# An adaLN and LoRA mixture feed-forward block: full-width warm-up matmuls, one engine for the lower rows' weights, and a last product that is stored bank by bank

## What is computed

```python
# layer 0
y = einsum('bct,bcd->bdt', x, cond_w[itok])          # mixes the 64 rows of each sequence
h = silu(y @ w1.T + b1) * (y @ w2.T + b2)            # up0, up1 (gate and up, 1024 each)
x = x + h @ w3.T + b3                                # down
# layer 1
z = x @ W + (x @ A[itok]) @ B[itok]                  # lin, with rank-16 LoRA
c = softmax((mean_s(z) @ Wq.T) @ keys.T / sqrt(128)) # 8 experts
x = x + z @ W_org.T + sum_e c[e] * (z @ down[e]) @ up[e]   # exp, expup
```

## Time and profile before

| | |
|---|---|
| median of 3 runs | 1001.23 us (1001.08 to 1001.4) |
| the profiled execution | 999.71 us |
| its span in the trace | 998.0 us |
| TensorE matmul busy | 989.2 us, 99% |
| VectorE busy | 743.1 us, 74% |
| ScalarE busy | 391.3 us, 39% |
| GpSimd busy | 39.1 us, 4% |
| granted TensorE clock, mean | 0.999 |

### The profile page before, as it was taken

One profiled execution on the slowest core, in us unless ns is written; L12 is line 12 of the kernel. 1 busy time (PEld: TensorE's weight loads), 2 busy tenths in 40 slices (PEclk: granted clock), 3 DMA queues, 4 the chain that ended last, 5 costly groups with the idle time before them and its releaser, 6 DMA issues.

```text
span 998.0 us, 12355 instructions
## 1 busy us (share of the span) xinstructions
PE 989.2 (99%) x4768; PEld 815.9 (82%) x4768; DVE 743.1 (74%) x578; ACT 391.3 (39%) x349; POOL 39.1 (4%) x65
## 2 busy tenths in 40 slices
PE   8999999999999999999999999999999999999997
PEld 7888888888887888888898888888888878888886
DVE  2977977998866889674436888789885859878641
ACT  7553653543344333331055544543433532424110
POOL 2600000000000000000100000000000000000011
PEclk9999999999999999999999999999999999999999
DMA  9022044034014001425211211521330230031012
GB/s 356 3 91 100 1 166 171 22 108 167 1 43 155 14 1 64 164 90 180 115 43 43 84 43 46 208 85 33 119 145 2 84 127 0 1 106 43 1 64 106
DMA packets 22986, 84.68 MB, mean 85 GB/s; under 512 B 2691, under 2 KB 6803, under 8 KB 17043
## 3 DMA queue, kind: packets, MB, share of 16 engines
q1 hardware_dynamic: 20450, 75.24, 20.8%
q0 software_dynamic: 2400, 8.41, 2.2%
q10 hardware_dynamic: 80, 0.26, 0.1%
HBM read 75.51 MB, written 8.39 MB: 84 GB/s over the span
## 4 chain that ended last, share of the span: by engine, by line
PE 98%; issue 1%; DMA 0%; POOLq 0%; DVE 0%; POOL 0%; SPq 0%
PE banks L653 31%; PE banks L654 31%; PE banks L655 31%; PE banks L749 3%; PE banks L714 2%; PE banks L732 1%; DMA cond_sb<-cond_t_in 0%; DVE r L1017 0%; PE banks L762 0%; POOLq L1166 0%; POOL out_t L631 0%; PE banks L778 0%; POOL mix L464 0%; PE banks L772 0%; SPq L469 0%
## 5 line engine op out<-in xcount | busy, mean ns | idle before, releaser
L653 PE MATMUL banks<-s_hi,t_hi 128*128 128x512 f32 x1360 | 531.7, 391 | 0.0
L654 PE MATMUL banks<-s_lo,t_hi 128*128 128x512 f32 x1360 | 529.5, 389 | 0.0
L655 PE MATMUL banks<-s_hi,t_lo 128*128 128x512 f32 x1360 | 529.2, 389 | 0.0
L653 PEld LDWEIGHTS banks<-s_hi,t_hi 128*128 128x128 f32 x1360 | 255.3, 188 | 56.6 <-issue 3.8
L655 PEld LDWEIGHTS banks<-s_hi,t_lo 128*128 128x128 f32 x1360 | 255.3, 188 | 53.2
L654 PEld LDWEIGHTS banks<-s_lo,t_hi 128*128 128x128 f32 x1360 | 255.3, 188 | 52.5
L1017 DVE TENSOR_TENSOR r<-banks,r 128x1024 f32<-128x1024 f32 x92 | 111.4, 1219 | 97.7 <-PE banks L655 93.1
L919 DVE TENSOR_TENSOR t_lo<-w,t_hi 128x1024 fp32r<-128x1024 f32 x132 | 156.5, 1218 | 5.1 <-ACT t_hi L849 5.1
L830 ACT CAST s_hi<-st 128x2048 fp32r<-128x2048 f32 x40 | 76.5, 1913 | 198.0 <-PE banks L655 145.7
L849 ACT CAST t_hi<-w 128x1024 fp32r<-128x1024 f32 x132 | 133.3, 1048 | 49.0 <-PE banks L655 48.9
L830 ACT CAST s_hi<-r 128x2048 fp32r<-128x2048 f32 x34 | 65.0, 1913 | 203.3 <-PE banks L655 178.2
(11 more groups left out here) (70 smaller groups left out, 356.4 us busy)
## 6 DMA issues: line engine op xcount, KB each, us to landing
w<-w_up_in SPq DMA_DIRECT2D x16, 1024.0 KB, 4.8
w<-w_base_in SPq DMA_DIRECT2D x10, 1024.0 KB, 4.7
w<-w_down_in SPq DMA_DIRECT2D x8, 1024.0 KB, 5.4
r<-x_t_in SPq DMA_DIRECT2D x8, 1024.0 KB, 6.2
w<-w_lin_in SPq DMA_DIRECT2D x8, 1024.0 KB, 5.1
out_t<-r POOLq DMA_DIRECT2D x16, 512.0 KB, 3.2
we<-w_expin_in SPq DMA_DIRECT2D x10, 512.0 KB, 4.6
st<-x_pairs_in SPq DMA_DIRECT2D x8, 512.0 KB, 6.4
```

Source lines behind the costliest of these rows:

```text
L653: pe.matmul(out, w_hi, x_hi, start=start, stop=False, skip_group_check=True)
L654: pe.matmul(out, w_hi, x_lo, start=False, stop=False, skip_group_check=True)
L655: return pe.matmul(out, w_lo, x_hi, start=False, stop=stop, skip_group_check=True)
```

## The change

Three things change.

- VectorE first writes ones into an idle part of SBUF, 128 rows by 640 columns. TensorE runs three matmuls of ones on all 128 rows and 128 columns, 512 columns each, ahead of its wait for the zeroed parts of `mix`.
- The lower rows' weights of half 0 are all copied by VectorE, in eight copies that are written out instead of looped. ScalarE makes none. Both loads of `cond_t` are issued by SP, and x of pair 0 is issued by ScalarE's queue as its first instruction.
- The last product (`LAST`, product 3 of expup in half 1) is added bank by bank by VectorE and stored bank by bank by SP, 256 KB each.

```diff
-WARM = 2
+WARM = 3
@@ def dve_own(n):
+    if n == LAST:
+        return [[("add one", n, g) for g in groups_of(j)] for j in range(2)]
@@ build
+        ones = r[:, 5, 0:P + TN]
@@ sync_engine
-            sp.dma_start(cond_sb[S:P, :, :], cond_t).then_inc(cond_loaded, 16)
-            for c in range(4):
+            for j in range(2):
+                sp.dma_start(cond_sb[j * S:(j + 1) * S, :, :], cond_t).then_inc(cond_loaded, 16)
+            for c in range(1, 4):
                 load_x(0, c)
...
+            for g in range(4):
+                sp.wait_ge(summed, SUM_AT["add one", LAST, g])
+                sp.dma_start(out_t[4 + g, :, TOK:TOK + TN], group_block(LAST, g)).then_inc(stored_last, 16)
             for b in range(4):
-                sp.wait_ge(stored[b], HALVES * 2 * 16)
+                sp.wait_ge(stored[b], (2 if b == 1 else 4) * 16)
+            sp.wait_ge(stored_last, 4 * 16)
@@ pool_engine
-                for u in range(4):
+                for u in range(4 if h == 0 else 3):
                     store(h, u, 0)
                     store(h, u, 1)
@@ tensor_engine
+            pe.wait_ge(ones_made, 1)
+            for _ in range(WARM):
+                pe.matmul(banks[:, 7, :], ones[:, 0:P], ones[:, P:P + TN], start=True, stop=True)
             pe.wait_ge(mix_zeroed, 2)
-            for _ in range(WARM):
-                pe.matmul(banks[0:S, 7, :], mix[0:S, 0, S:P], mix[0:S, :, S:P], start=True, stop=True)
@@ scalar_engine
-            act.dma_start(cond_sb[0:S, :, :], cond_t).then_inc(cond_loaded, 16)
-            act.wait_ge(idx_loaded, 16)
-            make_mixing(act, act.copy, 0, [(1, 1)])
-
+            act.dma_start(x_pair(0), x_pairs[0]).then_inc(x_loaded[0], 16)
@@ vector_engine
+            dve.memset(ones, 1.0).then_inc(ones_made, 1)
             dve.memset(mix[0:S, :, S:P], 0.0).then_inc(mix_zeroed, 1)
             dve.memset(mix[S:P, :, 0:S], 0.0).then_inc(mix_zeroed, 1)
             dve.wait_ge(idx_loaded, 16)
-            make_mixing(dve, dve.tensor_copy, 0, [(0, 1)])
+            for c in range(PAIRS):
+                v = dve.value_load(idx_sb[0:1, 2 * c + 1:2 * c + 2], min_val=0, max_val=NCOND - 1)
+                if c == 0:
+                    dve.wait_ge(cond_loaded, 32)
+                dve.tensor_copy(mix[S:P, c, S:P], cond_sb[S:P, bass.ds(v, 1), :].rearrange("p a m -> p (a m)")).then_inc(
+                    mix_made[1 + c % 2], 1)
@@ take
+                    elif op == "add one":
+                        dve.wait_ge(group_done, GROUP_AT[n, at])
+                        dve.wait_ge(summed, SUM_AT["add", phase_of(h, "exp", ENDS[UP_TO_BLOCK[i]]), at // 2])
+                        dve.tensor_tensor(group_block(n, at), banks[:, bank_of(n, at), :], group_block(n, at),
                                           ALU.add).then_inc(summed, 1)
```

More of the change, by code:

```diff
@@ L312, in build @@
         wq_loaded = sem("wq_loaded")
-        mix_zeroed = sem("mix_zeroed")
+        ones_made, mix_zeroed = sem("ones_made"), sem("mix_zeroed")
         consts_made, masks_made = sem("consts_made"), sem("masks_made")
@@ L342, in build @@
         coef_full, coef_ready = sem("coef_full"), sem("coef_ready")
-        stored = [sem(f"stored{b}") for b in range(4)]
+        stored, stored_last = [sem(f"stored{b}") for b in range(4)], sem("stored_last")
         def first_block(h, own):
@@ L1017, in take @@
                         dve.tensor_tensor(half_block(n, at), half_banks(n, at), half_block(n, at),
+                                          ALU.add).then_inc(summed, 1)
+                    elif op == "add one":
+                        dve.wait_ge(group_done, GROUP_AT[n, at])
+                        dve.wait_ge(summed, SUM_AT["add", phase_of(h, "exp", ENDS[UP_TO_BLOCK[i]]), at // 2])
+                        dve.tensor_tensor(group_block(n, at), banks[:, bank_of(n, at), :], group_block(n, at),
                                           ALU.add).then_inc(summed, 1)
```

## The result

The changed kernel takes 996.70 us in the median of 7 runs (996.44 to 999.03). Two of the seven took 999.0, the other five 996.4 to 997.2. The kernel before took 1000.94 in the median of 7 runs (1000.71 to 1001.4). The ratio over all runs is 0.9966, with a 95% interval of 0.9956 to 0.9976, so 3.4 us less (2.4 to 4.4); the two medians are 4.2 apart, inside the same interval. The forecast was 998.0, with 996.9 to 999.8 as its range for the time. The prediction had 1001.23 as the median of before; against that the forecast stood at 3.2 us less.

What follows compares the result with a forecast made beforehand. The prediction took TensorE to bound the kernel, with gains only at its two ends: 1.3 us at the start plus 1.95 at the end, 3.25 off 1001.23, gives 998.0 us in the median, range 996.9 to 999.8.

Steps and rivals of the forecast that it cites:

- Where the time is: Whole kernel: TensorE is 98% of the chain, so only edits before the first product or after the last can pay.
- Part 1, the ones: Warm-up before half 0's mixing: three matmuls of ones bring it to full pace, 14.29 us instead of 16.17.
- this bound: The upper case for the warm-up: mixing starts at full pace; the lower case was mixing as slow as before.
- the sum: The forecast's calculation on the profiled execution: 1.3 us off at the start plus 1.95 at the end, 3.25 us.
- Part 2, the start: First mixing matmul, after the reordered loads: starts at 6.9 us, bounds 6.1 and 7.3; the move itself gains nothing.
- Part 3, pair 4 and s_lo: Before the first product: pair 4 waits for x until about 14.35 us, s_lo ends at 21.15, mixing at 21.53.
- start gain: Time by which the first product comes earlier: 1.29 us, taken as 1.3, bounds 0 and 1.7.
- Part 4, VectorE's copies: Half 0's lower-row weights: eight VectorE copies at 1.3 us each stay ahead of TensorE and cost nothing.
- The rival that forecast a slower kernel from T = 2.5 us: VectorE's load and copy, T each, starve mixing; at T = 3.0 the time is 1005 us; chance 0.04.
- Part 5, the tail: Last add to program end: 3.61 us instead of 5.56, a gain of 1.95, bounds 1.1 and 2.6.
- the extra 1.52 us: Timed median of before, 1001.23, over its profiled execution, 999.71: carried unchanged, so a saving counts in full on the median.

Runs made afterwards that it cites:

- experiments 1: The kernel before with only the three full-width matmuls of ones added in place of its narrow warm-ups: 999.37 us, ratio 0.9983.
- Experiment 5: The changed kernel with its three warm-up matmuls of ones cut to 64 rows and 64 columns: 998.49 us, ratio 0.9983.
- experiment 4: The changed kernel with the loads as before (cond_t from ScalarE's and SP's queues, then x of pair 0 from SP): 997.19 us, ratio 0.9959.
- experiment 3: The kernel before with only the last product's banks added and stored one by one by SP: 998.86 us, ratio 0.9977.
- experiment 7: On top of experiment 4, x of pairs 4 and 5 issued before the first weight block, t_hi and t_lo moved behind s_hi: 996.48 us, ratio 0.9961.
- experiment 2: The kernel before with only the new load order and VectorE's eight written-out copies, narrow warm-ups kept: 1000.67 us, ratio 0.9997.
- Experiment 11: The changed kernel with the last product added and stored in two pairs of banks, still by SP: 998.02 us, ratio 0.9975.

## Why the prediction was right

- **Where the time is.** Right. Only the two ends changed, and their sum is the difference of the spans.
- **Part 1, the ones.** The forecast was right, and experiments 1 and 5 show it: the ones bring the mixing to full pace, 1.6 us. The reason given for choosing this bound was not: it leaned on the gap of a microsecond that would close. Experiment 5 has nearly the changed kernel's gap (0.76 us against 0.62) and its length and stays slow; experiment 4 has a gap of 1.81 and is at full pace. Between experiment 5 and the changed kernel only the width differs, so for narrow ones the same argument would have forecast a gain that isn't there. The rule cited from the Trainium skill, which speaks of activity and not of width, doesn't cover this by itself. The matmuls of ones took 5.42 us where the sum had 5.5 as its upper end.
- **Part 2, the start.** The step failed in its bound. It gave 6.1 to 7.3 and took 6.9; the mixing started at 7.76, because cond_t, now second to x, landed at 7.1, 1.6 us later than before. That comes from the change: with the loads of before, cond_t landed at 5.3 to 5.6 in five profiles. The start itself moved less. With the loads of before, the mixing began at 7.64, 7.47, 7.93 and 7.42 in four other profiles (experiments 1, 3, 4 and 7), and 6.89 was the exception; with the new order it began at 7.45 to 8.10 in seven. The means are 7.47 and 7.82, so of the 0.87 us some 0.35 may be the change and the rest is the execution; the two ranges overlap. That the move gives nothing either way was right as far as the timed runs can tell (experiment 2, 0.9997). The Trainium skill's rule that the two queues share the DMA engines held: in experiments 2 and 4 the earlier load of the one was paid for by the other (x at 4.6 and cond_t at 6.9, cond_t at 5.3 and x at 7.8).
- **Part 3, pair 4 and s_lo.** The mechanism is real: pair 4 waits for x in experiments 1 and 4, and the wait goes in experiment 7. In the changed kernel's profile it didn't bind, since with a start at 7.76 pair 4's turn came at 14.87, and its x had landed at 14.5. The start gain was 0.77 us in place of 1.29: from the start of the mixing to the first product it took 14.29 us instead of 15.93, and 0.87 of these 1.64 us were lost again by the later start. The sum had let a start up to 7.2 cost nothing. s_lo ended at 21.4, before the mixing, as forecast.
- **Part 4, VectorE's copies.** Right, and the price was over-estimated: 0.76 us a copy (eight from 7.3 to 12.6), not 1.3. The rival that forecast a slower kernel from T = 2.5 us had no ground.
- **Part 5, the tail.** Add 0.69 as taken, SP's answer 0.03 as taken, landing 2.1 in place of 2.4. The gain was 2.22 in place of 1.95. The fit cited from the Trainium skill gave 2.6 for the landing; it is one for GpSimd's queue, and for SP's store the trace is half a microsecond below it. Experiment 11 splits the gain: 1.03 us for the queue, 1.19 for the size.
- **The median.** The step that the extra 1.52 us of the timed runs carry over unchanged was wrong. The profiled execution of before had its x early (6.7 against 7.3 to 7.8 in other profiles with the same loads), so it had less to gain than a usual run. In the changed kernel the median run is the profiled one. Between the two profiles the sum was 0.25 us too high (3.25 against 3.0); between the medians it was too low (3.25 against 3.4 by the ratio, 4.2 by the medians), and the time came 1.3 us under the forecast. Of the 1.2 us from the profiled execution of before (999.71) to the median (1000.94) the early loads explain about 0.6: experiments 2 and 3, with the mixing at 7.45 and 7.47, have their first product at 23.45 and 23.39 instead of 22.82. The rest is open. The other timed runs of before have no profile, and in experiment 3, whose loads were not early, the profiled run is still 0.8 us below the median.

## What to carry to other kernels

Warm TensorE up with matmuls on the full array: matmuls on a quarter of it for as long did nothing visible here. At the end of a program, add and store the last piece alone and from SP; half of the gain is the smaller piece, half the queue. And before a bound of a tenth of a per cent is worked out from one execution, look whether its first loads landed where those of other executions do, because that alone moved the start by 1 us here. An order of loads that only swaps which one is last won nothing.

## What the runs showed of the hardware that was not expected

- In ten profiles with full-width ones the first 64 records of mixing took 7.4 us; in four with 64 by 64 warm-ups they took 9.0 to 9.1. The granted clock is printed as 1.00 in all these stretches, at full pace as at half pace: the column reads 1.00 also ahead of the clock's first rise (10.4 us in the kernel before, 6.9 in the changed one), so there only the pace of the records tells the level.
- From 2 to 7 us the transfers move 257 to 300 GB/s in the 14 profiles, with the DMA engines busy for 0.89 to 0.98 of it; later, as in 9 to 10 of the changed kernel, it is 414. The 512 KB of pair 0, third on the queues, landed anywhere from 6.7 to 7.8 us. This varies from execution to execution and moves the start of the mixing.
- A register load and a small copy on VectorE, written out, take 0.76 us a turn against 1.3 in the hardware loop of the kernel before.
- ScalarE's first activation-table load now stands at 1.26, ahead of its first wait, and costs nothing. In the loop of the kernel before it loaded the table ahead of each of its four copies, 1.28 us each.
